# Bank copies on ScalarE and every sixth layer-2 square there, in a two-layer graph kernel in fp32

## What is computed

```python
h  = relu(layernorm(x)) @ W0 + B0
M  = (adj < 0.5) & ~eye
S  = where(M, exp(-(1/adj - 1/mu)**2 / (2*sigma**2)), 0)
x1 = x + S @ h                                  # layer 1
h2 = relu(layernorm(x1)) @ W1.T
y  = x1 + (adj*adj + eye) @ h2                  # layer 2
```

## Time and profile before

| | us |
|---|---|
| median of 3 runs | 1846.52 (1845.3 to 1847.08) |
| the profiled execution | 1844.98 |
| its span, first to last instruction | 1842.8 |
| TensorE busy | 1817.3 |
| ScalarE busy | 1744.2 |
| VectorE busy | 1734.3 |
| GpSimd busy | 94.3 |
| granted TensorE clock, mean over the span | 0.994 |

### The profile page before, as it was taken

How to read it: one execution, slowest core, us unless ns; L and a number is a source line. 1 busy time by engine, 2 the same in 40 slices (tenths; PEclk the granted TensorE clock), 3 DMA queues, 4 the chain that set the end, 5 groups by cost and what they waited for, 6 DMA issues and landing times.

```text
span 1842.8 us, 13474 instructions
## 1 busy us (share of the span) xinstructions
PE 1817.3 (99%) x4860; PEld 886.6 (48%) x4860; DVE 1734.3 (94%) x1045; ACT 1744.2 (95%) x1010; POOL 94.3 (5%) x117
## 2 busy tenths in 40 slices
PE   7989999999999999999999999999999999999998
PEld 4544444444444444444444444444444444556675
DVE  8999999999999999999999999999999986889897
ACT  8999999999999999999999999999999999889774
POOL 0000001000000000000000000000000000000011
PEclk8999999999999999999999999999999999999999
DMA  8477889888988788777877677677666658966998
GB/s 318 166 301 265 328 299 316 303 319 276 330 272 323 270 294 296 267 264 293 285 253 271 225 260 267 239 262 272 244 253 223 234 226 290 322 255 249 306 363 252
DMA packets 85441, 509.12 MB, mean 276 GB/s; under 512 B 9856, under 2 KB 10496, under 8 KB 28032
## 3 DMA queue, kind: packets, MB, share of 16 engines
q1 hardware_dynamic: 70128, 478.77, 68.6%
q0 software_dynamic: 15104, 29.37, 8.9%
q10 hardware_dynamic: 144, 0.13, 0.0%
HBM read 478.61 MB, written 29.62 MB: 276 GB/s over the span
## 4 chain that ended last, share of the span: by engine, by line
PE 91%; ACT 6%; DVE 1%; issue 1%; DMA 0%; DVEq 0%
PE p_x L493 26%; PE p_l1b L459 23%; PE p_l1a L459 21%; PE p_own L493 12%; ACT rings L825 2%; ACT rings L830 2%; ACT rings L835 2%; PE p_x L471 1%; PE p_x L473 1%; PE p_x L472 1%; PE p_proj L544 1%; PE p_stat L535 1%; PE p_own L471 1%; PE p_own L472 1%; PE p_own L473 1%
## 5 line engine op out<-in xcount | busy, mean ns | idle before, releaser
L635 DVE SCALAR_TENSOR_TENSOR rings<-rings,small 128x2048 f32<-128x2048 f32 x256 | 600.1, 2344 | 20.8 <-ACT rings L830 20.6
L628 DVE SCALAR_TENSOR_TENSOR rings<-rings 128x2048 f32<-128x2048 f32 x256 | 584.6, 2284 | 16.2 <-PE p_l1b L459 14.3
L835 ACT ACTIVATE rings<-rings,small 128x2048 f32<-128x2048 f32 x256 | 533.0, 2082 | 29.8 <-DVE rings L635 29.5
L493 PE MATMUL p_x<-rings,h 128*128 128x512 f32 x1128 | 506.1, 592 | 0.0
L825 ACT ACTIVATE rings<-rings 128x2048 f32<-128x2048 f32 x256 | 485.6, 1897 | 10.4 <-DVE rings L628 8.0
L830 ACT ACTIVATE rings<-rings 128x2048 f32<-128x2048 f32 x256 | 487.7, 1905 | 5.1
L459 PE MATMUL p_l1b<-rings,h 128*128 128x512 f32 x1024 | 460.1, 595 | 0.0
L459 PE MATMUL p_l1a<-rings,h 128*128 128x512 f32 x1024 | 458.1, 593 | 1.1 <-DVE h L697 1.1
L493 PEld LDWEIGHTS p_x<-rings,h 128*128 128x128 f32 x1128 | 214.3, 190 | 266.6 <-issue 265.5
L459 PEld LDWEIGHTS p_l1b<-rings,h 128*128 128x128 f32 x1024 | 194.4, 191 | 236.2 <-issue 234.2
L459 PEld LDWEIGHTS p_l1a<-rings,h 128*128 128x128 f32 x1024 | 193.0, 190 | 233.5 <-issue 229.6
(11 more groups left out here) (95 smaller groups left out, 598.1 us busy)
## 6 DMA issues: line engine op xcount, KB each, us to landing
rings<-adjT SPq DMA_DIRECT2D x448, 1024.0 KB, 6.9
outT<-xa_buf POOLq DMA_DIRECT2D x96, 256.0 KB, 7.2
x_buf<-xT SPq DMA_DIRECT2D x24, 256.0 KB, 5.4
outT<-y_buf POOLq DMA_DIRECT2D x15, 256.0 KB, 7.3
xa_buf<-xT SPq DMA_DIRECT2D x8, 256.0 KB, 5.4
outT<-x_buf POOLq DMA_DIRECT2D x1, 256.0 KB, 4.9
y_buf<-outT SPq DMA_DIRECT2D x1, 256.0 KB, 13.8
outT<-y_buf SPq DMA_DIRECT2D x1, 128.0 KB, 1.8
```

Source lines behind the costliest of these rows:

```text
L493: last = pe.matmul(out[:, :], h2[:, it.source * G + g, :], block_of(a_ring, it.load % A_RING, g), start=(it.first and g == 0), stop=(it.la ...
L628: dve.scalar_tensor_tensor(out=tile(s_ring, slot_of(t)), in0=tile(a_ring, slot), scalar=CUTOFF, in1=tile(a_ring, slot), op0=ALU.is_lt, op1 ...
L635: dve.scalar_tensor_tensor(out=v, in0=v, scalar=neg_2c, in1=v, op0=ALU.add, op1=ALU.mult).then_inc(squared, 1)
L835: act.activation(v, v, ACT.Exp, bias=exp_bias, scale=neg_k).then_inc(sens_done, 1)
```

## The change

In all steps ahead of the last chunk the bank of a finished chain is copied by ScalarE (an activation of the kind Copy, PSUM to SBUF) in place of VectorE. It stands after the logarithm of the step and ahead of the row steps. The steps of the copies are the same, and so are the buffers, the stores and all matmuls. In the last chunk and after it VectorE copies as before; its first copy there waits for the count of all ScalarE copies. Ahead of step 240, ScalarE squares the items with m divisible by 6 in place of 3, and VectorE the rest.

```diff
-        it.by = "act" if it.m % 3 == 0 and it.row != it.source else "dve"
+        it.by = "act" if it.m % 6 == 0 and it.row != it.source else "dve"
...
+EARLY_CHAINS = sum(len(chains) for chains in EVAC_AT.values())
...
             def add_chain(ch):
...
+                if k == EARLY_CHAINS:
+                    dve.wait_ge(xa_added, k)
                 dve.tensor_copy(buf[:, :], p_chain[ch.bank][:, :]).then_inc(xa_added, 1)
...
             for s in range(STEPS + 8):
...
-                for ch in EVAC_AT.get(s, []):
-                    add_chain(ch)
...
+            def copy_chain(ch):
+                k = ch.index
+                act.wait_ge(q_used, ch.last_m + 1)
+                if k >= XA_RING:
+                    act.wait_ge(xa_stored[k % XA_RING], 16 * (k // XA_RING))
+                elif k >= 2:
+                    act.wait_ge(node_centred, NC)
+                act.activation(xa_buf[k % XA_RING][:, :], p_chain[ch.bank][:, :], ACT.Copy).then_inc(xa_added, 1)
...
                 if s < S_STEPS and not dense:
                     log(s)
+                for ch in EVAC_AT.get(s, []):
+                    copy_chain(ch)
                 if c >= 1:
                     row_steps(s)
```

## The result

The kernel after takes 1848.49 us (median of 22 runs, 1846.57 to 1849.57), the kernel before 1845.36 (22 runs, 1844.31 to 1848.52). The ratio is 1.0013 with a 95% interval of 1.0007 to 1.0019, so +2.4 us (1.3 to 3.5). That is slower, by more than the noise of 22 runs, but by less than the 0.2% up to which the prediction calls two times the same. The prediction said +1.5 and 1848.0. An execution's time has 1.8 us around its span here, and 2.2 in the kernel before, so the spans differ by 0.4 us more than the times do.

The account below looks back on a forecast made before the run. TensorE was taken to bound the kernel from chunk 2 to the edge of the last chunk. Two chunk 1 waits, 1.1 + 0.4 = +1.5 us, on the median 1846.52 gave 1848.0, range 1845 to 1854, "same" at 0.75.

Parts of the forecast that it names:

- What bounds the kernel: From chunk 2 to the edge of the last chunk only TensorE's own work counts; TensorE has no idle time there.
- Loads and prices: Whole kernel: VectorE +17.5 us to about 1752 busy, ScalarE −14.0 to 1730; a ScalarE copy takes 0.576 us.
- The absolute time, 1848.0: Whole kernel: +1.5 us added to 1846.52, the median of three runs of the kernel before.
- The walk through chunk 1: Chunk 1, steps 24 to 31: ScalarE's copies make TensorE lose 1.1 us at step 24 and 0.4 in step 28.
- From chunk 2 on TensorE is 1.5 us later than before, which widens every other margin.: From chunk 2 on: TensorE's 1.5 us delay from chunk 1 gives the other engines that much more margin.
- Chunk 2's price: Chunks 2 to 5: VectorE 392.4 and ScalarE 396.5 of 402.3 us, both fit, so cost 0.
- waits for banks beyond 2 us in sum: Sign of being wrong: TensorE's waits for banks add up to more than 2 us.
- none behind it: Sign of being right: after TensorE's waits on copies near 158 and 186 us, no more until the last chunk.
- Rival 1: Chunks 6 to 14: VectorE becomes the bound if idle there above 10.5 us; TensorE waits some 17 us, 1865; 18%.
- Rival 2: Clock: the new 1.1 us TensorE wait lowers the clock as the longer wait did, 1.7 us more, 1849.7; 6%.
- second dip: Sign of being wrong: the clock dips a second time near 160 us.
- Rivals 3 and 4: 3: TensorE isn't the bound, time follows ScalarE, 1832.5, 5%. 4: copies need table loads, ScalarE busy 1904, 2%.

## Why the prediction was right, and where it was short

- **What bounds the kernel: right.** Over 1306 us the kernel before has no idle time of TensorE, and no variant was faster. The Trainium skill's busy share of the weight loads ("Perfetto Trace Analysis", Identifying the Most-Contended Engine), taken alone, would have had it the other way; the section asks for MFU beside it, which was not worked out. ScalarE's load fell by 13.6 us and nothing was gained.
- **Loads and prices: right**, to 2.4 us on each engine over the whole span and 0.001 us on the copy.
- **The absolute time, 1848.0 against 1848.49: in part luck.** It was built on a median of three runs, 1846.52, where 22 runs give 1845.36. That is 1.2 us too high, and covered most of the chunk-2 term that was missing.
- **The walk through chunk 1: right.** 1.16 and 0.29 us against 1.1 and 0.4, at the forecast items. The 0.1 us that each wait costs behind it was not in the sum.
- **The step that failed: "From chunk 2 on TensorE is 1.5 us later than before, which widens every other margin."** VectorE's x1 waits for TensorE in step 35 (0.57 us of it before, 2.40 and 2.52 with the change), so all engines shift by what TensorE lost in chunk 1. Chunk 2's price was put at nothing, judged by its sums of busy time, which say nothing of the moment at which a bank is due. One sign that the prediction had named for being wrong did come: "waits for banks beyond 2 us in sum" (2.73), and "none behind it" failed with the wait in chunk 2. The trace of the kernel before had the answer. Its ScalarE and TensorE in step 43:

```profile
282.47 1.89 ACT L825 ACTIVATE rings<-rings 128x2048 f32<-128x2048 f32 x1
```

```profile
283.91 3.60 PE L493 MATMUL p_x<-rings,h 128*128 128x512 f32 x8
```

  282.47 + 1.81 + 0.58 = 284.86 for the end of ScalarE's copy, 0.95 us behind the 283.91 at which TensorE wants the bank. Measured: 1.28 to 1.30, since ScalarE's copies in the steps ahead push its own logarithm back as well (283.71 with the change in chunk 2 only, where TensorE is 0.93 later: 0.3 more than that). With this term the sum is 1.1 + 0.4 + 1.0 = 2.5 us, against 2.73 of waits in the trace and 2.4 by the ratio.
- **Rival 1 (VectorE the bound): it did not come, but it was near.** VectorE's idle time in chunks 6 to 14 is 9.4 us, where 10.5 was the point from which it decides, and the lead of the exponential at the start of chunk 14 is down from 2.6 us to 0.4 (1437.09 + 2.08 = 1439.17, TensorE at 1439.60):

```profile
1437.09 2.08 ACT L837 ACTIVATE rings<-rings,small 128x2048 f32<-128x2048 f32 x1
```

- **Rival 2 (the clock): no second dip.** The granted clock is 1.00 in the window with the 1.28 us wait (285 to 290 us). But the first dip was of different length in two executions of the same program, and moved one wait.
- **Rivals 3 and 4** fell: nothing was faster, and the copies ran at the price of an instruction.

What stays open: 0.9 to 2.8 us of ScalarE's lateness in chunks 4 and 5 is seen in four variants and follows the lead at chunk 4 in three of them, but was not taken apart into copies and the order of row steps.

## What to carry to other kernels

Where three engines are full to 94% and more, a sum of busy times shows only that a move is not ruled out; the cost sits in single due times, and for a step that is moved behind another one they can be read from the trace of before, in every chunk and not only in the first. Whether a delay of the bounding engine gives the others a lead depends on whether one of them waits for it in between: VectorE does at the start of chunk 2, and chunk 1's delay gave no lead; it waits only 0.29 us at chunk 3 and not at all at chunks 4 to 6, and of chunk 2's delay 1.0 us became a lead there. And a wait that is taken away pays only as far as the next engine's margin reaches: here 2.7 us of waits were removed, and by the ratios 1.1 to 2.6 us remained.

## What the runs showed of the hardware that was not expected

The same program, with the same wait of 2.6 us near 132 us, had the lower clock for different lengths: a granted clock of 0.58, 0.50 and 0.96 from 135 to 146 us in one execution, 0.77, 0.75 and 1.00 in another of the same kernel. A dip of this kind followed a wait of 2.0 us too: in the kernel with the squares alone, TensorE idles 2.03 us up to 387.5, and the window behind it stands at 0.61, in the middle of full work. The tile behind that wait takes 392.70 − 387.47 = 5.23 us in place of 3.43.

```profile
388.00:392.00 4.00, 4.00 (x7) 1.73 (x6) 4.00 (x3) 3.97 (x3) 0.00 (x0) 0.61 1.01 337
```

The waits of 1.1 to 1.3 us in the other runs left it at 1.00, and so did one of 1.79 us in this one, up to 903.8.
